# The last feed-forward block: the wide norm's sums move from DVE to ACT, its factor to ACT and its bias to Pool

## The reference, cut to what matters

```python
def layernorm(x, g, b):
    mu = jnp.mean(x, axis=-1, keepdims=True)
    var = jnp.mean((x - mu) ** 2, axis=-1, keepdims=True)
    return (x - mu) * jax.lax.rsqrt(var + LN_EPS) * g + b
def act_quant_fake(x):
    scale = 127.0 / jnp.clip(jnp.max(jnp.abs(x), axis=-1, keepdims=True), 1e-05)
    return jnp.clip(jnp.round(x * scale), -128.0, 127.0) / scale
h = layernorm(x, ln1_g, ln1_b)
h = bitlinear(h, w1, b1)                 # 256 -> 1024, quantized x and ternary w1
h = jax.nn.gelu(h, approximate=False)
h = layernorm(h, ln2_g, ln2_b)           # over 1024: the "wide norm"
h = bitlinear(h, w2, b2)                 # 1024 -> 256
x = _layernorm(x + h, axis=-1)           # over 256: the output
```

## Time and profile before

| | |
|---|---|
| median of three runs | 2312.98 us |
| the profiled execution: its own time | 2315.36 us |
| its span | 2313.6 us |
| the last stage within it | about 2008 to 2313.6 us |
| busy in 2100 to 2200 us, of 100 us | DVE 92.73, PE 57.27, ACT 40.83, POOL 28.84 |
| granted clock of PE in the same stretch | 0.70 |
| busy over the whole span | DVE 77%, PE 76%, ACT 58%, POOL 37% |

### The profile page before, as it was taken

One profiled execution on the slowest core, in us unless ns is written; L12 is line 12 of the kernel. 1 busy time (PEld: TensorE's weight loads), 2 busy tenths in 40 slices (PEclk: granted clock), 3 DMA queues, 4 the chain that ended last, 5 costly groups with the idle time before them and its releaser, 6 DMA issues. The chain is left out here.

```text
span 2313.6 us, 36269 instructions
## 1 busy us (share of the span) xinstructions
PE 1758.1 (76%) x12104; PEld 1097.3 (47%) x12104; DVE 1782.5 (77%) x4542; ACT 1333.4 (58%) x3347; POOL 847.5 (37%) x983
## 2 busy tenths in 40 slices
PE   8939999999968777775666666665899999556564
PEld 4503333333336566664444554434577667433333
DVE  4668888888626888885888888845578787599997
ACT  1204666666733344342078888899999992144443
POOL 2420000000007768753333333300575775323232
PEclk9957999999967989896777777767899999866766
DMA  2001111111020010000000000010000000000000
GB/s 79 19 21 29 30 30 30 30 28 29 12 63 15 12 31 13 12 6 19 1 19 1 1 1 1 1 35 23 1 19 1 1 1 1 30 12 16 14 15 18
DMA packets 42807, 41.54 MB, mean 18 GB/s; under 512 B 16054, under 2 KB 34670, under 8 KB 42622
## 3 DMA queue, kind: packets, MB, share of 16 engines
q1 hardware_dynamic: 42622, 39.23, 6.4%
HBM read 22.03 MB, written 4.19 MB: 11 GB/s over the span
## 5 line engine op out<-in xcount | busy, mean ns | idle before, releaser
L763 ACT ACTIVATE ST<-ST,aexp 128x1 f32<-128x1 f32 x2046 | 581.9, 384 | 2.0 <-PEq L57 2.0
L597 ACT ACTIVATE PT<-PS 128x512 f32<-128x512 f32 x576 | 309.8, 597 | 219.5 <-PE PS L482 188.6
L558 DVE CUSTOM_DVE_ANT_0 junk<-PS,maskw 128x128 bf16<-128x128 f32 (+3 forms) x512 | 226.5, 486 | 33.8 <-PE PS L459 33.8
L459 PE MATMUL PS<-KT,QT 48*128 48x512 bf16 (+3 forms) x768 | 190.1, 351 | 54.1 <-DMA QT<-QS 33.0
L561 DVE TENSOR_REDUCE MX<-PS 128x1 f32<-128x512 f32 x256 | 164.6, 685 | 27.7 <-PE PS L459 24.9
L501 PE MATMUL PS<-PT,VP 128*32 128x256 f32 (+1 forms) x2560 | 184.2, 370 | 0.0
L94 PE MATMUL PS<-ident,X 128*128 128x128 f32 x256 | 64.0, 339 | 143.7 <-DVE X L128 129.6
L631 POOL TENSOR_SCALAR nm<-MX 128x16 f32<-128x16 f32 x32 | 6.5, 203 | 431.1 <-DVE MX L564 431.1
L1663 PE MATMUL PS<-L_xattn_VW,l_pT 112*128 112x256 f32 x704 | 157.4, 379 | 2.9 <-issue 2.9
L459 PEld LDWEIGHTS PS<-KT,QT 48*128 48x128 bf16 x768 | 58.4, 94 | 200.0 <-issue 80.3
L1648 PE MATMUL PS<-Q,l_xT 128*128 128x512 f32 (+1 forms) x384 | 144.1, 526 | 1.7 <-DVE l_s L1696 1.7
(11 more groups left out here) (317 smaller groups left out, 4502.5 us busy)
## 6 DMA issues: line engine op xcount, KB each, us to landing
KT<-KS SPq DMA_DIRECT2D x192, 32.0 KB, 2.0
QT<-QS SPq DMA_DIRECT2D x192, 32.0 KB, 2.0
xs<-in_x SPq DMA_DIRECT2D x8, 512.0 KB
cx<-in_x SPq DMA_DIRECT2D x32, 128.0 KB, 2.0
out<-j_xn SPq DMA_DIRECT2D x32, 128.0 KB, 1.7
QT<-NMT SPq DMA_DIRECT2D x192, 2.0 KB
f_raw<-in_L_ffn_w SPq DMA_DIRECT2D x2, 1024.0 KB, 5.5
j_raw<-in_L_ffn_w SPq DMA_DIRECT2D x2, 1024.0 KB, 5.3
```

The lines of the kernel that those rows point to most:

```text
L459: T.matmul(bank(u % 3)[:, 0:w * P], QT[i % R][rows, qt * P:(qt + 1) * P], KT[i % R][rows, k0 * P:(k0 + w) * P], start=True, stop=True).the ...
L558: V.tensor_tensor_reduce(junk[u % 3][:, 0:w * P], bank(u % 3)[:, 0:w * P], maskw[:, BANK - w * P:], 1.0, NEG, ALU.add, ALU.max, MX[i % 2][ ...
L597: C.activation(PT[n % 4][:, 2 * pr + e, 0:w], bank(3 + u % 3)[:, 0:w], ACT.Exp, scale=0.25).then_inc(e_done, 1)
L763: C.activation(self.ST[:, m, t:t + 1], self.ST[:, m, t - 1:t] if t else self.zero[:, :], ACT.Tanh, bias=self.BU[:, m, t:t + 1], scale=self ...
```

## The change

All of it lies in `ffn1`.

- ACT's Gelu gives as a second output the sum over the 1024 elements (`total`); a small operation on ACT makes of it the negative mean (`nm`). A further ACT operation, Square with nm as bias, gives the sum of squared differences (`sq`); its wide result goes to `junk` (bf16) and is not used. DVE makes `ve` of sq in one small operation. The statistics and moments of the wide norm on DVE are gone.
- DVE's hn = (h + nm) x g stays on DVE. The multiplication by the factor rs is a separate operation on ACT (`C.mul`, in place), and the bias is added by Pool (in place). DVE's L1892 is gone.
- The wide norm is one step longer: now a = j, b = j - 1, c = j - 2, d = j - 3, e = j - 4, and PE's, DVE's, ACT's and Pool's texts are reordered: DVE begins a step with h(b) and ends it with the third norm of e; ACT goes copy(a), Gelu(b), nm(b), t2(d), the product(c), Square(b), hqT(d); PE does the first product of a before the transposes of d; Pool goes xb(a), power(c), bias(c), power(e).
- Each of the four vectors has a semaphore of its own, the one for h is loaded first, and each is waited for where it is first used.

```diff
+        bh_in, g2_in, b2_in, bo_in = vec_in = st.sems("bh_in g2_in b2_in bo_in")
-        n2, n3, q2 = Norm(st, ctx, "n2", HID), Norm(st, ctx, "n3", D), Quant(st, ctx, "q2")
+        n3, q2 = Norm(st, ctx, "n3", D), Quant(st, ctx, "q2")
         def sp():
-            for d, n in ((g2_, "ln2_g"), (b2_, "ln2_b"), (bh, "b1"), (bo, "b2")):
-                SP.dma_start(d[:, :], row("L1_ffn_" + n)).then_inc(vec_in, 16)
+            for (d, n), landed_ in zip(((bh, "b1"), (g2_, "ln2_g"), (b2_, "ln2_b"), (bo, "b2")), vec_in):
+                SP.dma_start(d[:, :], row("L1_ffn_" + n)).then_inc(landed_, 16)
...
         def dve():
-            V.wait_ge(vec_in, 64)
...
+            for j in range(NT + 4):
+                b, c, d, e = j - 1, j - 2, j - 3, j - 4
+                if on(b):
+                    if b == 0:
+                        V.wait_ge(bh_in, 16)
+                        V.wait_ge(j_ds, 1)
+                    V.wait_ge(j_mm, b + 1)
+                    V.scalar_tensor_tensor(h[b % 3][:, :], bank(1 + 2 * (b % 2), 2), ds[:, b:b + 1], bh[:, :], ALU.mult, ALU.add).then_inc(j_h, 1)
                 if on(d):
                     V.wait_ge(j_l2b, d + 1)
                     q2.dve_max(d, hn[d % 3][:, :])
...
+                if on(c):
+                    V.wait_ge(j_sq, c + 1)
+                    V.tensor_scalar(ve[c % 3][:, :], sq[c % 3][:, :], 1.0 / HID, EPS, ALU.mult, ALU.add).then_inc(j_ve, 1)
+                    if c == 0:
+                        V.wait_ge(g2_in, 16)
+                    if c >= 3:
+                        V.wait_ge(j_t2, c - 2)
+                    V.scalar_tensor_tensor(hn[c % 3][:, :], h[c % 3][:, :], nm[c % 3][:, :], g2_[:, :], ALU.add, ALU.mult).then_inc(j_l2g, 1)
                 if on(e):
...
-                if on(c):
-                    V.wait_ge(j_gelu, c + 1)
-                    n2.dve_stats(c, h[c % 3])
...
-                if on(c):
-                    V.wait_ge(n2.rstd_done, c + 1)
-                    V.wait_ge(j_l2g, c + 1)
-                    V.scalar_tensor_tensor(hn[c % 3][:, :], hn[c % 3][:, :], n2.rs[c % 4][:, :], b2_[:, :], ALU.mult, ALU.add).then_inc(j_l2b, 1)
...
         def act():
...
+                if on(a):
+                    C.wait_ge(j_tr, a + 1)
+                    if a >= 2:
+                        C.wait_ge(j_mm, a - 1)
+                    C.copy(xqT[a % 2][:, :], bank(0).bitcast(BF16)[:, 0:D]).then_inc(j_xqT, 1)
+                if on(b):
+                    C.wait_ge(j_h, b + 1)
+                    if b >= 3:
+                        C.wait_ge(j_l2g, b - 2)
+                    C.activation(h[b % 3][:, :], h[b % 3][:, :], ACT.Gelu, accum_out=total[b % 3][:, :]).then_inc(j_gelu, 1)
+                    C.wait_ge(j_gelu, b + 1)
+                    C.mul(nm[b % 3][:, :], total[b % 3][:, :], -1.0 / HID).then_inc(j_nm, 1)
                 if on(d):
...
+                if on(c):
+                    C.wait_ge(j_l2g, c + 1)
+                    C.wait_ge(j_rs, c + 1)
+                    C.mul(hn[c % 3][:, :], hn[c % 3][:, :], rs[c % 3][:, :]).then_inc(j_us, 1)
                 if on(b):
...
+                    C.wait_ge(j_nm, b + 1)
+                    if b >= 3:
+                        C.wait_ge(j_ve, b - 2)
+                    C.activation(junk[:, :], h[b % 3][:, :], ACT.Square, bias=nm[b % 3][:, :], scale=1.0, accum_out=sq[b % 3][:, :]).then_inc(j_sq, 1)
...
         def pool():
-            G.wait_ge(vec_in, 64)
+            G.wait_ge(bo_in, 16)
+            for j in range(NT + 4):
+                a, c, e = j, j - 2, j - 4
                 if on(a):
                     if a >= 6:
                         G.wait_ge(n_y, a - 5)
                     G.tensor_tensor(xb[a % 6][:, :], X[:, a, :], bo[:, :], ALU.add).then_inc(j_xb, 1)
+                if on(c):
+                    G.wait_ge(j_ve, c + 1)
+                    G.tensor_tensor(rs[c % 3][:, :], ve[c % 3][:, :], neghalf[:, :], ALU.pow).then_inc(j_rs, 1)
+                    if c == 0:
+                        G.wait_ge(b2_in, 16)
+                    G.wait_ge(j_us, c + 1)
+                    G.tensor_tensor(hn[c % 3][:, :], hn[c % 3][:, :], b2_[:, :], ALU.add).then_inc(j_l2b, 1)
+                if on(e):
+                    n3.pool_rstd(e)
```

More of the change, by code:

```diff
@@ L1805, in ffn1 @@
         y, xn = ring(ctx, "j_y", 2, [P, D]), ring(ctx, "j_xn", 4, [P, D])
-        vec_in, consts, j_xb, j_ds, j_tr, j_xqT, j_mm, j_h, j_gelu = st.sems("vec_in consts xb ds tr xqT mm h gelu")
+        total, nm, sq, ve, rs = (ring(ctx, f"j_{n}", 3, [P, 1]) for n in ("total", "nm", "sq", "ve", "rs"))
+        junk = sb(ctx, "j_junk", [P, HID], BF16)
+        consts, j_xb, j_ds, j_tr, j_xqT, j_mm, j_h, j_gelu = st.sems("consts xb ds tr xqT mm h gelu")
+        bh_in, g2_in, b2_in, bo_in = vec_in = st.sems("bh_in g2_in b2_in bo_in")
         j_l2g, j_l2b, j_t2, j_ds2, j_hqtr, j_hqT, j_mm2, n_y, n_xn = st.sems(
             "l2g l2b t2 ds2 hqtr hqT mm2 y xn")
+        j_nm, j_sq, j_ve, j_rs = st.sems("nm sq ve rs")
+        j_us, = st.sems("us")
         out_st = st.slots("out_st", 4)
-        n2, n3, q2 = Norm(st, ctx, "n2", HID), Norm(st, ctx, "n3", D), Quant(st, ctx, "q2")
+        n3, q2 = Norm(st, ctx, "n3", D), Quant(st, ctx, "q2")
         def on(i):
@@ L1824, in pe @@
         def pe():
-            for j in range(NT + 2):
-                b, d = j, j - 2
+            for j in range(NT + 3):
+                a, d = j, j - 3
+                if on(a):
+                    if a >= 1:
+                        T.wait_ge(j_xqT, a)
+                    transposes(JQ[:, a, :], bank(0).bitcast(BF16), KD).then_inc(j_tr, 1)
+                    T.wait_ge(j_xqT, a + 1)
+                    if a >= 2:
+                        T.wait_ge(j_h, a - 1)
+                    for c in range(2):
+                        for k in range(KD):
+                            last = T.matmul(bank(1 + 2 * (a % 2) + c), xqT[a % 2][:, k * P:(k + 1) * P],
+                                            w1.wT[:, k, c * BANK:(c + 1) * BANK], start=k == 0, stop=k == KD - 1)
+                    last.then_inc(j_mm, 1)
                 if on(d):
@@ L1831, in pe @@
                     transposes(t2[d % 2], bank(5, 2), KH).then_inc(j_hqtr, 1)
[L1832 to L1845, removed]
                     T.wait_ge(j_hqT, d + 1)
@@ L1855, in dve @@
             V.memset(down[:, :], -MAGIC).then_inc(consts, 1)
-            V.wait_ge(vec_in, 64)
             V.tensor_scalar(ds[:, :], LV[:, :], w1.scale[:, :], None, ALU.mult).then_inc(j_ds, 1)
-            for j in range(NT + 3):
-                b, c, d, e = j, j - 1, j - 2, j - 3
+            for j in range(NT + 4):
[6 more added lines that the diff above has]
+                    V.scalar_tensor_tensor(h[b % 3][:, :], bank(1 + 2 * (b % 2), 2), ds[:, b:b + 1], bh[:, :], ALU.mult, ALU.add).then_inc(j_h, 1)
                 if on(d):
@@ L1870, in dve @@
                     V.scalar_tensor_tensor(y[e % 2][:, :], bank(7)[:, 0:D], ds2[e % 4][:, :], xb[e % 6][:, :], ALU.mult, ALU.add).then_inc(n_y, 1)
-                if on(c):
-                    V.wait_ge(j_gelu, c + 1)
-                    n2.dve_stats(c, h[c % 3])
-                if on(e):
                     V.wait_ge(n_y, e + 1)
                     n3.dve_stats(e, y[e % 2])
-                if on(c):
-                    n2.dve_moments(c)
-                if on(e):
                     n3.dve_moments(e)
[L1881 to L1884, removed]
                 if on(e):
@@ L1888, in dve @@
                     n3.dve_apply(e, xn[e % 4][:, :], y[e % 2][:, :]).then_inc(n_xn, 1)
-                if on(c):
-                    V.wait_ge(n2.rstd_done, c + 1)
-                    V.wait_ge(j_l2g, c + 1)
-                    V.scalar_tensor_tensor(hn[c % 3][:, :], hn[c % 3][:, :], n2.rs[c % 4][:, :], b2_[:, :], ALU.mult, ALU.add).then_inc(j_l2b, 1)
[L1893 to L1896, removed]
         def act():
             C.wait_ge(consts, 1)
-            for j in range(NT + 2):
-                b, d = j, j - 2
+            for j in range(NT + 3):
+                a, b, c, d = j, j - 1, j - 2, j - 3
+                if on(a):
+                    C.wait_ge(j_tr, a + 1)
+                    if a >= 2:
+                        C.wait_ge(j_mm, a - 1)
[7 more added lines that the diff above has]
+                    C.mul(nm[b % 3][:, :], total[b % 3][:, :], -1.0 / HID).then_inc(j_nm, 1)
                 if on(d):
@@ L1916, in act @@
                     C.activation(hqT[d % 2][:, :], bank(5, 2), ACT.Identity, bias=down[:, :], scale=1.0).then_inc(j_hqT, 1)
-                if on(b):
-                    C.wait_ge(j_h, b + 1)
-                    C.activation(h[b % 3][:, :], h[b % 3][:, :], ACT.Gelu).then_inc(j_gelu, 1)
         def pool():
-            G.wait_ge(vec_in, 64)
[L1923 to L1928, removed]
+            G.wait_ge(bo_in, 16)
+            for j in range(NT + 4):
+                a, c, e = j, j - 2, j - 4
                 if on(a):
```

## The result

Measured beside each other, the changed kernel takes 2328.41 us (median of 5, 2325.75 to 2330.17) and the kernel before 2316.10 us (median of 5, 2312.34 to 2318.57): 12.3 us more, ratio 1.0057, 95% interval 1.0045 to 1.0068. The forecast was 10.7 us more, 2323.7, with a range of 2308 to 2341. The profiled execution took 2330.17 us with a span of 2328.4.

The account below looks back on a forecast made before the run. DVE's own work, 8.4 of 8.93 us a step, bounds the kernel before; afterwards a loop through Pool takes 9.48. With start and end that is +10.7 us on the median of 2312.98: 2323.7, range 2308 to 2341.

Parts of the forecast that it names:

- The loop: From one h on DVE through hn(c), ACT's product, Pool's wide add and power of e, and xn: 9.48 us a step.
- xn to the next start: Last part of the step, DVE's xn(e) beside Pool's xb until the next DVE start: 0.66 us.
- some 7.7: Time in DVE's step at which the third norm's ve was expected, after Pool's wide add had started.
- Pool's wide add: Pool adding b2 to hn(c), 1024 elements: 2.33 us, bounded by 1.905 and 2.88; the term that decides.
- The held power: Pool's power of c beside DVE's hn(c): 1.52 us instead of 0.55, ending 0.40 after hn(c).
- The other engines: ACT's own loop through PE: 9.0 us a step with second outputs at half their bound, under 9.48.
- Start and end: First maximum 2.9 us earlier, last at 2311.2 against 2300.44, tail unchanged.
- the three xb on Pool: At the stage's start, three Pool operations of 0.72 us each ahead of its first power.
- neither 1.90: Rival: Pool's add runs like the repeated-column row, 1.90 us; no measurable change, 2309.9; chance 0.17.
- nor less: Rival: Pool's add is no slower than the DVE operation it replaces, 1.27 us; near -16, 2297; chance 0.07.
- Second outputs: Rival: ACT's second outputs cost 0.5 to 0.77 us each, above the 0.38 bound; 2330 to 2345; chance 0.07.
- Square shares a table with Gelu: Rival claimed the opposite: ACT loads a table twice a step, +62 to +74 us, 2375 to 2387; chance 0.04.

Follow-up runs that it names:

- Experiment 1: Changed kernel with Pool's power of e moved ahead of the wait for ACT's product and the wide add of c: 2296.17 us, ratio 0.9906.
- experiment 4: Experiment 1 with PE turning the next tile (a + 1) ahead of the transposes of d: 2295.41 us, ratio 0.9911.
- experiment 7: Changed kernel with xn one step later, PE turning tile a + 1 ahead of d's transposes, and ve(c) ahead of the maximum: 2277.12 us, ratio 0.9822.
- experiment 2: Changed kernel with ve(c) moved on DVE from behind the maximum's small operations to right behind h(b): 2315.13 us, ratio 0.9993.
- experiment 5: Changed kernel with xn one step later on DVE, y in four buffers, Pool's order untouched: 2285.33 us, ratio 0.9850.
- experiment 3: Changed kernel with two unused statistics of 512 elements added on DVE between the third norm's moments and xn: 2329.45 us, ratio 1.0054.
- experiment 9: Experiment 7 with xn(e - 1) moved on DVE to right behind hn(c), ahead of y(e): 2244.08 us, ratio 0.9689.

## Why the prediction was right

- **The loop.** Predicted at 9.48 us a step, with 2.88 us from h to hn(c); measured 9.48 and 2.87 (2165.56 to 2168.43). Experiment 1 shows the cause by cutting it at one place. Term by term against the rows above: h to the power's end 4.55 (4.56 predicted), to the product 0.10 (0.07), the product 1.15 (1.15), to the add 0.07 (0.08), the add 2.34 (2.33), the power of e with its pauses 0.62 (0.63), xn to the next start 0.65 (0.66). The last of these terms holds something that the prediction did not see: xn takes 0.73 us there and 0.41 in the tail of before, and it ends 0.15 after Pool's xb (2174.39 + 0.73 against 2174.25 + 0.72), as the held xn of experiment 1 ends 0.15 after the wide add. It came out right because the row that it was taken from the earlier trace rows has the same neighbour.
- **A slip, and a gap, in the reasoning.** The third norm's ve was put at "some 7.7" us in the step; the prediction's own terms give 2.88 + 1.2 + 2.41, 6.5, and it was measured at 5.26 (2165.56 to 2170.82). It changes nothing, since the power stands behind the add either way. The same passage looks only for DVE operations with two SBUF tensors beside Pool's add. Experiments 1, 4 and 7 show that the one-input xn is held as well; in the changed kernel it stands behind the add, and so the sum was spared.
- **Pool's wide add.** The line through two rows of the same form gave 2.33, the run 2.34; the row of the same width but with a repeated column (1.905) would have given a forecast of no change, and the Trainium skill's factor from GPSIMD Engine Reference, "Performance versus the Vector engine", an estimate of 2.49, which the measured 2.34 doesn't bear out at this width. Same form at another size was the better guide than same size in another form.
- **The held power.** 1.52 us, as in the first step of before; experiment 2 shows that its neighbour hn(c) holds it.
- **The other engines.** ACT's loop was put at about 9.0 and is 8.16 in the long steps of experiment 5 (7.20 in the short ones), so its cover was right and its size too high. The mis-sized terms: nm costs its start to the next 0.11 in experiment 5 and not 0.38; Square with its second output 1.13 (2171.26 to 2172.39) and not 1.34; Gelu with its own 1.18 (2166.87 to 2168.05) and not 1.25; and from the second product's start to the copy 2.14 (PE's row at 2173.54) and not 2.42, for the transposes of bf16 follow closer. Had the Pool term been smaller, this error would have counted.
- **Start and end.** First maximum predicted 2.9 us earlier, measured 2.5 from the first issue. The term at fault is the three xb on Pool, 2.16 predicted: they took 3.07. In that time hn(0) ran on DVE, and hn(0) (2019.63 to 2020.94) has two SBUF tensors like the operation that holds the power; that it held the last xb is likely, but was not tested by itself. The tail is 13.2 us, as before. From first to last maximum it took 289.4 us, predicted 289.1. Some of this agreement is luck: the second distance between maxima was 10.58 and not 9.48, and the last three were 9.16, 7.98 and 7.97, where one of 9.48 and two of 8.29 were forecast. The two errors nearly cancel.
- **The median.** The forecast stood on 2312.98; the same kernel's median over five runs is 2316.10, and the forecast's 10.7 on that is 2326.8 against 2328.41. The 1.6 left over is within the spread of each kernel's own runs. So 3.1 of the 4.7 us by which the forecast of 2323.7 was low lie in the time of before and not in the change.
- **Rivals.** The add was neither 1.90 nor less. Second outputs cost 0.19 a row, under the bound. Square shares a table with Gelu: the groups of the changed kernel's last stage have a single load, as the earlier trace rows of before.

```profile
L1908 ACT ACT_TABLE_LOAD x1 | 1.3, 1283 | 0.0
```

That is what the Trainium skill's rule in ScalarE: Activation LUTs, "Table sets: the hidden batching unit", leads one to expect if Square is a cheap function; its list of gelu's set does not name it.

Where I went wrong was after the prediction: ACT's loop was thought to be next behind the Pool loop, and the first experiment's time agreed. A held instruction, counted as busy, was next. One more edit that should have paid and didn't (experiment 4) was needed to see it.

## What to carry to other kernels

Taking nearly a third of its work off the busiest engine gains nothing where the engine then waits, in every step, for a longer way through other engines; walk the loop from one start of an instruction to its next, through every in-order queue, and add up starts and pauses, before counting busy time. Put a short power or other small result that the bound engine waits for ahead of a long operation in the same queue, or use it one step later. And when a shortened loop doesn't get as short as it should, look for an instruction whose duration has grown beside a neighbour's: the page counts it as work.

## What the runs showed of the hardware

- Pool's add of two SBUF tensors (2.34 us) holds DVE's 256-element tensor_scalar from SBUF to SBUF (xn): 2.35 instead of 0.41 us where it starts 0.14 later, and 2.56 even where it starts 0.07 earlier (experiments 1, 4 and 7). Statistics (one input) and a one-element tensor_scalar beside the same add are not held (experiments 3 and 9). Why a start 0.07 ahead doesn't win was not tested and stays open. That the 0.73 us of xn beside the 0.72 of Pool's xb, in both kernels, is the same effect fits its end, 0.15 after xb's each time; no run moved xb to test it.
- The other way round, DVE's operation with two SBUF tensors holds Pool's power until 0.40 after its end: 1.52 instead of 0.55 us. Moved beside the one-input maximum it is not held (experiment 2).
- A second output of an activation is an instruction of 0.19 us behind it, which costs ACT about 0.1 behind Square (2172.30 to 2172.39 us) and 0.2 where the next one waits for it.
- PE's granted clock between 2100 and 2200 us was 0.70 before, 0.59 in the changed kernel and 0.78 in experiment 9, a mean of stretches at 1.2 and at 2.4 GHz. It shows in the step where the loop through PE is the limit: in experiment 5 it is 8.16 us from one maximum to the next where the eight matmuls of the second product took 1.89 us (from 2164.09, granted clock 0.50, that is 1.2 GHz), and 7.20 (2172.52 to 2179.72) in the next step, where they took 1.05 (from 2172.25, granted clock 1.00, 2.4 GHz) and the copy's wait was 1.25 instead of 2.19.
